# The Gram matrix of the channel attention, its second half of rows in 129 columns and a transposition

## The reference

```python
qkv = x @ w_qkv + b_qkv
q, k, v = jnp.split(qkv, 3, axis=-1)          # (B, L, 512) each, 8 heads of 64
scores = jnp.einsum('bhld,bhle->bhde', q, k) / jnp.sqrt(jnp.asarray(dx, x.dtype))
attn = jax.nn.softmax(scores, axis=-1)        # 64 x 64 for each head
out = jnp.einsum('bhld,bhde->bhle', v, attn)
out = out.transpose(0, 2, 1, 3).reshape(B, L, H * dx)
out = out @ w_fc + b_fc
```

## Time and profile before

| | us |
|---|---|
| median of 3 runs | 1524.97 |
| the profiled execution, its own time | 1530.72 |
| its span, first to last instruction | 1528.9 |
| TensorE busy | 1414.6 (93%) |
| VectorE busy | 1077.1 (70%) |
| ScalarE busy | 853.6 (56%) |
| GpSimd busy | 239.8 (16%) |
| mean granted TensorE clock | 0.96 |

### The profile page before, as it was taken

How to read it: one execution, slowest core, us unless ns; L and a number is a source line. 1 busy time by engine, 2 the same in 40 slices (tenths; PEclk the granted TensorE clock), 3 DMA queues, 4 the chain that set the end, 5 groups by cost and what they waited for, 6 DMA issues and landing times. The chain is left out here.

```text
span 1528.9 us, 43961 instructions
## 1 busy us (share of the span) xinstructions
PE 1414.6 (93%) x18420; PEld 875.8 (57%) x18420; DVE 1077.1 (70%) x1993; ACT 853.6 (56%) x1775; POOL 239.8 (16%) x380
## 2 busy tenths in 40 slices
PE   7879899999999899999999999899997569999998
PEld 4434344444434444444344444687876559999997
DVE  1366858888888888888888882355589446767675
ACT  2325537767767577677676776744455223333333
POOL 3212021111102111111021100000114501111111
PEclk9989999999999999999999999999996579999999
DMA  8555017612315114123210000300814354445441
GB/s 235 161 108 103 4 63 120 90 27 31 47 28 67 22 36 56 28 30 48 64 39 3 3 3 2 110 27 14 309 50 145 109 190 178 167 179 186 182 174 72
DMA packets 77824, 134.10 MB, mean 88 GB/s; under 512 B 12226, under 2 KB 64443, under 8 KB 72252
## 3 DMA queue, kind: packets, MB, share of 16 engines
q1 hardware_dynamic: 72412, 121.45, 30.9%
q0 software_dynamic: 3408, 8.43, 1.6%
q10 hardware_dynamic: 1808, 1.41, 0.3%
HBM read 67.77 MB, written 23.11 MB: 59 GB/s over the span
## 5 line engine op out<-in xcount | busy, mean ns | idle before, releaser
L1675 DVE TENSOR_REDUCE part_max<-pair 128x2 f32<-128x1024 f32 (+2 forms) x576 | 647.6, 1162 | 114.9 <-PE pair L1154 55.3
L1503 ACT ACTIVATE big<-pair 128x512 f32<-128x512 f32 (+1 forms) x1120 | 565.3, 610 | 243.0 <-PE pair L1175 240.6
L1148 PE MATMUL pair<-big 128*32 128x512 bf16 (+3 forms) x5120 | 359.1, 352 | 29.2 <-DVE part_max L1675 24.2
L1175 PE MATMUL pair<-big 128*32 128x512 bf16 (+3 forms) x5120 | 345.5, 352 | 6.8 <-DMA big<-max_t 3.6
L1197 PE MATMUL pair<-big 128*17 128x512 f32 (+3 forms) x2560 | 280.2, 528 | 1.5 <-issue 1.0
L1148 PEld LDWEIGHTS pair<-big 128*32 128x32 bf16 x5120 | 134.9, 97 | 198.9 <-DVE part_max L1675 100.0
L1175 PEld LDWEIGHTS pair<-big 128*32 128x32 bf16 x5120 | 126.6, 96 | 178.3 <-ACT big L1503 88.9
L1516 ACT ACTIVATE std<-moments,eps_col 128x1 f32<-128x1 f32 (+1 forms) x110 | 32.4, 295 | 226.0 <-DVE moments L1713 221.9
L2039 POOL TENSOR_SCALAR_AFFINE_SELECT big<-big 128x512 f32<-128x512 f32 x128 | 79.8, 636 | 477.9 <-ACT big L1503 477.9
L1411 PE MATMUL pair<-big,tok 128*128 128x128 f32 x1248 | 147.5, 277 | 3.0 <-DVE big L1939 2.9
L1411 PEld LDWEIGHTS pair<-big,tok 128*128 128x128 f32 x1248 | 146.4, 193 | 6.5 <-DVE big L1939 4.7
(11 more groups left out here) (160 smaller groups left out, 1262.3 us busy)
## 6 DMA issues: line engine op xcount, KB each, us to landing
tok<-big SPq DMA_DIRECT2D x39, 1024.0 KB
big<-in_L_ffn_w SPq DMA_DIRECT2D x16, 1024.0 KB
big<-split_dram SPq DMA_DIRECT2D x216, 64.0 KB, 4.7
split_dram<-big SPq DMA_DIRECT2D x32, 384.0 KB, 2.7
big<-split_dram SPq DMA_DIRECT2D x42, 256.0 KB, 6.2
big<-routed_dram SPq DMA_DIRECT2D x39, 129.0 KB, 2.1
tok<-in_L_attn_x SPq DMA_DIRECT2D x8, 512.0 KB, 9.4
big<-in_c_query_rows SPq DMA_DIRECT2D x8, 512.0 KB, 5.3
```

Source lines behind the costliest of these rows:

```text
L1148: mm = pe.matmul(bank[q:q + STRIPE, o:o + w], m.q_op[slot][:, step.qt, h, step.r * P + q:step.r * P + q + STRIPE], m.k_op[slot][:, h, step ...
L1175: mm = pe.matmul(m.bank[step.bank][k:k + STRIPE, n * w:(n + 1) * w], m.k_op[slot][:, h, step.kb * P + k:step.kb * P + k + STRIPE], m.q_op[ ...
L1503: act.activation(m.p_ring[:, step.place, step.heads[0]:step.heads[-1] + 1, step.at:step.at + w], m.bank[step.bank][:, 0:len(step.heads) * ...
L1675: dve.tensor_reduce(m.part_max[(step.u * QT + step.qt) % 2][:, step.r, step.heads[0]:step.heads[0] + n, step.c], banks[:, :, 0:w], X, ALU. ...
```

## The change

The second half of the rows (features 128 to 255) is multiplied with the columns 128 to 256 alone, 129 in place of 257; the second half's columns 0 to 127 are the transposed block of the first half's columns 128 to 255. That block is turned on TensorE (`GramTurn`, one transposition of 128 x 128, into the bank of the second half) and copied by ScalarE into `gram`. `GramK` part 1, the first that reads the block, waits for it; part 0 reads the column sums only. The planner's cost of a Gram step goes from 900 to 690.

```diff
-                yield "pe", Gram(batch, i, None), 900, [("end", "S", (batch * BPB + i) // BPT)] + free, ("gram", batch)
+                yield "pe", Gram(batch, i, None), 690, [("end", "S", (batch * BPB + i) // BPT)] + free, ("gram", batch)
             yield "dve", GramCopy(batch), 420, [("gram", batch)], ("gram 0", batch)
             yield "act", GramCopy(batch), 420, [("gram", batch)], ("gram 1", batch)
+            yield "pe", GramTurn(batch), 300, [("gram 0", batch), ("gram 1", batch)], ("gram turned", batch)
+            yield "act", GramTurn(batch), 380, [("gram turned", batch)], ("gram 2", batch)
             yield "pe", GramK(batch, 0), 1800, [("gram 0", batch), ("gram 1", batch)], ("gram k", batch, 0)
-            yield "pe", GramK(batch, 1), 1800, [], ("gram k", batch, 1)
+            yield "pe", GramK(batch, 1), 1800, [("gram 2", batch)], ("gram k", batch, 1)
...
             for half, b in enumerate(FOLD_BANKS):
-                mm = pe.matmul(m.bank[b][:, 0:D + 1], m.tok[:, blk, half * P:(half + 1) * P], m.tok[:, blk, 0:D + 1],
-                               start=(step.i == 0), stop=(step.i == BPB - 1))
+                mm = pe.matmul(m.bank[b][:, 0:D + 1 - half * P], m.tok[:, blk, half * P:(half + 1) * P],
+                               m.tok[:, blk, half * P:D + 1], start=(step.i == 0), stop=(step.i == BPB - 1))
...
+        elif isinstance(step, GramTurn):
+            pe.wait_ge(s.gram_by_dve, step.batch + 1)
+            pe.wait_ge(s.gram_by_act, 2 * step.batch + 1)
+            pe.transpose(m.bank[b1][:, 0:P], m.gram[:, 0, P:D], m.ident[:, :]).then_inc(s.gram_turned, 1)
...
             if step.part == 0:
                 pe.wait_ge(s.gram_by_dve, step.batch + 1)
-                pe.wait_ge(s.gram_by_act, step.batch + 1)
+                pe.wait_ge(s.gram_by_act, 2 * step.batch + 1)
...
+            if step.part == 1:
+                pe.wait_ge(s.gram_by_act, 2 * step.batch + 2)
...
             act.wait_ge(s.grammed, step.batch + 1)
-            act.activation(m.gram[:, 1, :], m.bank[b1][:, 0:D + 1], ACTF.Copy).then_inc(s.gram_by_act, 1)
+            act.activation(m.gram[:, 1, P:], m.bank[b1][:, 0:P + 1], ACTF.Copy).then_inc(s.gram_by_act, 1)
+
+        elif isinstance(step, GramTurn):
+            act.wait_ge(s.gram_turned, step.batch + 1)
+            act.activation(m.gram[:, 1, 0:P], m.bank[b1][:, 0:P], ACTF.Copy).then_inc(s.gram_by_act, 1)
```

More of the change, by code:

```diff
@@ L497 @@
 GramCopy = namedtuple("GramCopy", "batch")
+GramTurn = namedtuple("GramTurn", "batch")
 GramK = namedtuple("GramK", "batch part")
@@ L1029, in __init__ @@
         self.grammed, self.gram_by_dve, self.gram_by_act = sem("grammed"), sem("gram_by_dve"), sem("gram_by_act")
+        self.gram_turned = sem("gram_turned")
         self.gram_k_done, self.gram_k_set = sem("gram_k_done"), sem("gram_k_set")
@@ L1805, in vector_back @@
             if step.part == 0:
-                dve.wait_ge(s.gram_by_act, step.batch + 1)
+                dve.wait_ge(s.gram_by_act, 2 * step.batch + 1)
                 dve.scalar_tensor_tensor(m.gram_k_row, m.bk_wide[0:1, :], float(LENGTH), m.bank[b][0:1, :], ALU.mult,
```

## The result

The changed kernel takes 1517.45 us in the median of 15 runs, the kernel before 1524.04 in 15; the ratio is 0.9966, with a 95% interval of 0.9958 to 0.9975, so 3.8 to 6.4 us less; the two medians themselves lie 6.6 us apart. The forecast was 1517.6, a gain of 7.4 taken from 1524.97, the median of the first three runs. The time came out to 0.2 us; the gain here is smaller than forecast. The profiled execution took 1521.04 us, with a span of 1519.3. That is 9.6 us under the span of before, more than the times say. Single executions of one kernel lie 6 to 7 us apart here, so the profiles are read for where a difference sits, and the times for how large it is.

What follows compares the result with a forecast made beforehand. TensorE, busy 93% of the span, was taken to set the pace through all 32 Gram steps. Terms -7.0 + 0.4 + 0 + 0 - 0.8 = -7.4 us took 1524.97 to 1517.6, range 1512 to 1523.

Steps and rivals of the forecast that it cites:

- Gram steps: TensorE, second half: 64 passes fall from 0.217 to 0.107 us each, 7.0 us saved.
- Transpositions and waits: TensorE: one transposition per batch, two passes each, adds 0.4 us; GramK 1's 0.8 us wait for ScalarE is covered, 0.
- The batch 1 copy: VectorE, batch 1: the planner puts the Gram copy ahead of Second; cost 0, otherwise 1.4 us.
- The order: TensorE's list, batch 0: the 2.60 us hole before HeadTurn closes, new holes open; net 0.8 us gained, batch 1 unchanged.
- wrong if the first holds and the last does not: Back of kernel: prediction fails if second-half passes come 0.107 us apart but ChannelBias 1 to the experts changes over 1 us.
- Pass-through: Back of the kernel: TensorE's saving before 1140 moves all that follows, experts included; VectorE has about 3 us in 10 free.
- A: TensorE's order: the saving arrives, but the order gives nothing or costs up to 2.2 us; 1518.4 to 1520.6, chance 0.22.
- B: TensorE's clock: one more fall to 1.2 GHz costs about 3.4 us, giving 1521.0; chance 0.09.
- C: VectorE, full from 1140, absorbs the saving, so time stays at 1525; chance 0.12 shared with the narrow-passes-no-faster rival.
- D: TensorE: narrow passes no faster, 0.190 us loads set the pace; 1523.7, chance 0.12 shared with the VectorE-absorbs rival.
- E: Tail: one more late route adds 7.15 us, with GramK 1 waiting in both batches 2.0; 1526.8, chance 0.10.
- The time before: Whole kernel: profiled execution 5.75 us above the median of the runs; the same difference carried over to the changed kernel.

Runs made afterwards that it cites:

- the 65 columns: Changed kernel's order, second half multiplied with 65 columns in place of 129 for all but each batch's first block: 1517.1 against 1523.08 us, ratio 0.9967 to before.
- The fourth corner: Kernel before, its order and all 257 columns kept, with the transposition and its copy added: 1525.8 against 1526.66 us, ratio 1.000.
- the corners: Columns crossed with order, ratios to before: 257 columns 1.000 (old order), 1.0006 (new); 129 columns 0.9949 and 0.9959 (old), 0.9966 and 0.9937 (new).
- The second profile of before: The unchanged kernel before, profiled once more: 1524.44 us.

## Why the prediction was right

*Gram steps.* Four of them take 2.79 us, and 2.63 from their start to the start of the `Turn` behind them (1014.11 to 1016.74), so 0.657 us each, against 4 x 0.217 = 0.868 before: 0.211 a step, 6.8 us for 32. The term was 7.0. A pass of 129 columns takes 0.112 us, not 0.107. The sum took 0.30 for the duration of a transposition, which the profiles show as 0.27; with that its nearest row gives 0.110. That nothing is to be had below about 128 columns was right, as the 65 columns show; the recorded 190 ns of a load is no pace. That it is the load that sets this floor fits, but is not separated here: no run changed the load, and each of these passes has one of 128 columns.

*Transpositions and waits.* 0.4 and 0 were forecast. The 0.4 took each transposition for two passes; it is one, so the term by the same row is 0.2, and the traces show 0.2. The fourth corner shows nothing beyond 2.4 us, and there is no hole ahead of `GramK` 1 with ScalarE's copy in third place behind the transposed tile's copies. The turned block was there 1.02 us after the start of the transposition, where 0.8 was forecast; no row shows the 0.1 of signalling in it. `GramK` 0 covered both.

*The batch 1 copy.* VectorE copied at 1099.60, ahead of `Second` at 1099.94, as forecast. With both halves narrow in the order of before the copy stood behind `Second`, and 1.44 us showed, as forecast for that case.

*The order.* Most of the hand-worked list came out: 8, 4, 4 Gram steps and a `Multiply` over the head softmax; `Turn` S4 came ahead of `HeadScores` and `Multiply` O5 behind it. The step from there to a price was wrong in its form. I took batch 1 "as unchanged in its holes", and it is there that the new list lost. With wide passes batch 0 has 3.8 us less of holes and is spared a slow `Multiply` (5.41 us against 3.62). Batch 1 has 4, 8, 4 Gram steps, 2.6 us more of holes, and `FoldFc` and the `Turn` behind it at a low clock, 2.8 us more. That leaves about 0.2 us gained, and a `Turn` and an `Affinity` of 2.6 us that now come ahead of `ChannelBias` 1, so that the new list reaches it 2.5 us later than the old one. Behind it, where I had expected the same distance within 1 us, the changed kernel has 5.6 us less, and `ChannelBias` 1 is 5.9 us nearer to the first Gram step, not 7 (and 1.9 of the 5.9 are the slow stretch of the first profile of before). By the prediction's own sign ("wrong if the first holds and the last does not") this part failed: the saving did not arrive in the way described. The 0.8 us for the order is within what the corners can tell on the first chip, but it was the difference of gains and losses that I had not foreseen, and the second chip shows 3.8. That the time came out to 0.2 us is luck: the interval of the ratio alone is 2.6 us wide.

*Pass-through.* "A saving before 1140 should therefore move all that follows" held, for this change: of the 6.6 us that TensorE was spared, 5.3 to 6.8 arrived at `ChannelBias` 1. That was nearly all there was to have: the next 6.6 brought 1.8 at most. The 3 us in 10 that VectorE had free were an average, and were no measure of how much earlier the norms can come that each Gram step needs.

*The rivals.* A (nothing from the order) describes the corners on the first chip best. B: the clock fell in other places. 1040 to 1050 has 1.00 where it had been 0.93, and 1110 to 1120 has 0.92 where it had been 0.67 in the first profile of before, but 1.00 in the second. It fell behind the new hole instead (`FoldFc` at 1120.27 took 3.78 us for 8 passes): 0.74 in 1120 to 1130, where it had been 0.99 and 1.00. That is the sign that was named for B, but as one fall in place of another, the one behind the 2.60 us hole. C (kept off the end) was wrong for this change and nearly right for a cut of twice the size. D is ruled out. E: three routes came after VectorE ran dry in both orders, so it did not decide; its price of 7.15 us for a route is 6.1 in the changed kernel.

*The time before.* The 5.75 us between profile and median I carried along as one difference. The second profile of before took 6.3 us less: its first Gram step starts at 999.54 in place of 1004.07, so 4.5 us lie in the stages ahead of the change, and 1.9 are the clock behind `HeadScores` of batch 1.

## What to carry to other kernels

In long rows of float32 passes with 128 x 128 weights, columns could be dropped down to about 128 with gain (0.217 us for 257, 0.112 for 129), and no further (0.106 for 65 as for 8). Take the pace from a row of the same kind: the six passes of a group of `HeadScores`, of 128 columns too, take 1.06 us, 0.18 each, for a reason that no run here shows. Before a second cut of the same kind is built, leave the work out and see if the time moves: here 6.6 us more of TensorE's work gone brought 0 to 1 us. An engine that is busy 10 of 10 us may be only a few us ahead of the next chain. And where a planner's cost changes with the work, run the new work in the old order and the old work in the new one, since the two can hide each other, and do it on more than one chip: here the sign of the order changed from one to the next.

## What the runs showed of the hardware

**GpSimd holds up small steps of VectorE.** VectorE's shift of 128 x 4 elements took 0.16 to 0.22 us in 419 of 448 cases, over the back of all 14 profiles. The other 29 took 0.45 to 2.18 us. Each of these 29 started while a `ShiftBeta` of GpSimd was running (a TENSOR_TENSOR of 128 x 1024, 2.2 to 2.9 us) and ended 0.01 to 0.03 us behind it, and none of the 419 overlaps with one. VectorE's add of two operands of 128 x 1024 took 1.23 us, and 3.08 to 3.23 in the 12 cases in which it started during a `ShiftBeta`. So a step of 0.16 us can cost two microseconds by its place beside GpSimd alone, and in the row at 1084.25 above it did so on the path to TensorE. The profile shows the long step as busy, not as a wait, and names no releaser.

**Two chips, one kernel.** With the same lists the part from `ChannelBias` 1 to the experts took 92.6 us on one chip and 98.8 on another, 5.1 us of it in the wait for the transfers behind the last route. The waits of the routes that are named only "issue" or "remote" are there in all three profiles of wide passes in the order of before. What delays either is open.
